# Ten multiplications of the identity by itself behind the second pair of scores in a delta-rule recurrence

## The reference

```
def step(S, inp):
    q_i, k_i, u_i, w_i = inp
    attn_i = q_i @ jnp.swapaxes(k_i, -1, -2) * mask_causal
    u_new = u_i - w_i @ S
    o_i = q_i @ S + attn_i @ u_new
    S = S + jnp.swapaxes(k_i, -1, -2) @ u_new
    return (S, o_i)
S, o = jax.lax.scan(step, S0, (to_front(q), to_front(k), to_front(u), to_front(w)))
...
o = mix * o + (1.0 - mix) * v_token
o = o * jax.lax.rsqrt(jnp.mean(o * o, axis=-1, keepdims=True) + EPS) * norm_w
```

## Time and profile before

| | us |
|---|---|
| median of 3 runs | 2300.25 |
| lowest and highest | 2298.44, 2302.13 |
| the profiled execution, its own time | 2308.04 |
| its span | 2306.2 |
| PE busy | 2047.9 |
| DVE busy | 1347.8 |
| ACT busy | 1047.4 |
| POOL busy | 631.9 |

### The profile page before, as it was taken

The page is one execution under the profiler, slowest core; times in us unless marked ns, Lnnn a source line. Parts: engine busy times, 40 slices in busy tenths (PEclk is TensorE's granted clock), DMA queues, the critical chain, the costliest instruction groups (busy, mean ns, idle before and its releaser), DMA issues. The chain is left out here.

```text
span 2306.2 us, 46308 instructions
## 1 busy us (share of the span) xinstructions
PE 2047.9 (89%) x18079; PEld 1373.9 (60%) x18079; DVE 1347.8 (58%) x3476; ACT 1047.4 (45%) x2516; POOL 631.9 (27%) x720
## 2 busy tenths in 40 slices
PE   4989999987779999698857897958999999999998
PEld 2556666656666676454535555644666666666565
DVE  2017777743545555456536883135876777766677
ACT  4235655542244444312234445344666666666322
POOL 3015930002110000103762014552333333333100
PEclk9989999987869999799965558968999999999999
DMA  2036030002010000231251013430000000000000
GB/s 66 19 27 25 2 38 2 2 18 56 13 52 3 1 1 1 81 126 22 40 135 38 2 31 90 64 88 25 1 1 1 1 1 1 1 1 2 5 14 19
DMA packets 118326, 64.37 MB, mean 28 GB/s; under 512 B 65848, under 2 KB 113248, under 8 KB 116960
## 3 DMA queue, kind: packets, MB, share of 16 engines
q1 hardware_dynamic: 106128, 52.37, 10.0%
q0 software_dynamic: 11264, 8.66, 2.6%
q10 hardware_dynamic: 720, 0.40, 0.1%
HBM read 37.54 MB, written 23.86 MB: 27 GB/s over the span
## 5 line engine op out<-in xcount | busy, mean ns | idle before, releaser
L3000 ACT ACTIVATE l_prob<-l_ps,l_neg_max 128x128 f32<-128x128 f32 (+1 forms) x512 | 208.2, 419 | 49.8 <-DVE l_neg_max L3101 45.0
L1621 ACT ACTIVATE l0a_prob<-l0a_pst 128x1024 f32<-128x1024 f32 x128 | 131.0, 1024 | 119.9 <-PE l0a_pst L1539 119.9
L2885 POOL TENSOR_TENSOR l_prob<-l_prob,l_total 128x256 f32<-128x256 f32 x128 | 78.4, 612 | 372.0 <-DVE l_total L3109 372.0
L1672 DVE TENSOR_REDUCE l0a_peak<-l0a_ps 128x4 f32<-128x1024 f32 x128 | 156.2, 1221 | 16.0 <-PE l0a_ps L1534 14.0
L1534 PE MATMUL l0a_ps<-l0a_k,l0a_q 32*128 32x256 f32 x1024 | 146.6, 406 | 3.0 <-ACT l0a_prob L1621 2.5
L644 ACT ACTIVATE l0e_hidden<-l0e_ph,l0f_b 128x512 f32<-128x512 f32 x128 | 87.9, 687 | 129.2 <-PE l0e_ph L555 129.1
L3097 DVE TENSOR_TENSOR l_ps<-l_ps,future 128x512 f32<-128x512 f32 x128 | 89.4, 698 | 97.3 <-PE l_ps L2931 97.0
L1539 PE MATMUL l0a_pst<-l0a_q,l0a_k 32*128 32x256 f32 x1024 | 145.8, 400 | 0.2 <-ACT l0a_prob L1621 0.2
L565 PEld LDWEIGHTS l0e_py<-l0f_w,l0e_hidden 128*128 128x128 f32 x1024 | 119.7, 192 | 35.0 <-ACT l0e_hidden L644 32.7
L2886 POOL TENSOR_TENSOR l_prob<-l_prob,l_total 128x512 f32<-128x512 f32 x128 | 133.0, 1039 | 0.0
L565 PE MATMUL l0e_py<-l0f_w,l0e_hidden 128*128 128x128 f32 x1024 | 129.8, 280 | 0.3 <-ACT l0e_hidden L644 0.3
(11 more groups left out here) (518 smaller groups left out, 4815.2 us busy)
## 6 DMA issues: line engine op xcount, KB each, us to landing
l_band<-zero SPq DMA_DIRECT2D x16, 272.0 KB, 6.1
x_tok<-in_x_dram SPq DMA_DIRECT2D x2, 2048.0 KB, 8.1
l2f_w<-in_L_ffn_w_dram SPq DMA_DIRECT2D x2, 2048.0 KB, 10.0
l_rows<-l_band SPq DMA_DIRECT2D x16, 256.0 KB
l1f_w<-in_L_ffn_W_dram SPq DMA_DIRECT2D x3, 1024.0 KB, 12.0
l2x_rows<-l2x_sent SPq DMA_DIRECT2D x8, 288.0 KB, 5.1
gd_tri<-gp_tri SPq DMA_DIRECT2D x8, 256.0 KB, 2.0
l0f_w<-gd_tri SPq DMA_DIRECT2D x8, 256.0 KB, 13.3
```

The source lines that it names most:

```text
L1621: act.activation(prob[:, (n // 2) % 2, pair, :, :].rearrange("p g t s -> p g (t s)"), pst[:, :, :, :].rearrange("p g t s -> p g (t s)"), A ...
L1672: dve.tensor_reduce(to, ps[m % 2][:, :, :, :], AX.X, ALU.max, negate=True).then_inc(max_ready, 1)
L3000: act.activation(prob[:, m % 4, h, cols], ps[m % 2][:, h, cols], ACT.Exp, bias=neg_max[:, m % 4, h, t:t + 1], accum_out=total[:, m % 4, h, ...
```

## The change

A helper issues `count` matmuls of the identity by the identity into a bank. It is called once in each of the seven steps that have a next chunk, behind the second pair of scores and ahead of TensorE's wait for VectorE. Each call makes ten matmuls into the first quarter of the bank `pu`. Nothing reads what they write: the next matmuls into that bank are those of `values`, which start it anew.

```
+def keep_busy(pe, c, bank, count):
+    for _ in range(count):
+        pe.matmul(bank[:, :], c.ident[:, :], c.ident[:, :], start=True, stop=True)
...
                     if t + 1 < CH:
                         pe.wait_ge(attn_saved, HEADS * (t + 1) + 2)
                         scores(t + 1, 2)
+                        keep_busy(pe, c, pu[:, 0, :], 10)
                         pe.wait_ge(attn_saved, HEADS * (t + 1) + 4)
                         if t + 2 < CH:
                             to_tokens(t + 2)
```

## The result

| | before | changed |
|---|---|---|
| median of 12 runs, us | 2301.17 | 2292.54 |
| lowest and highest | 2293.84, 2305.81 | 2287.94, 2296.33 |
| profiled execution, its own time | 2308.04 | 2292.7 |

The ratio is 0.9968, with a 95% interval of 0.9956 to 0.9981: 4 to 10 us are saved, 8.6 by the medians. The forecast was 2291.6.

The account below looks back on a forecast made before the run. PE bounds the kernel, its clock falling in each recurrence step between transposes and state matmuls. Terms -12.7 + 0.8 + 3.2 = -8.7 us, from the median 2300.25 to 2291.6 us; range 2287.0 to 2297.5.

Parts of the forecast that it names:

- a clear gain: Whole program: faster by more than 4.6 us (0.2%), chance 0.76.
- The clock's ceiling: From the transposes to the state's matmuls, seven steps: at most 12.7 us saved if all 33.2 slow busy us went.
- What falls take back: In the seven steps: two to three clock falls remain, late in a gap behind dense work, 1.3 us each, 3.2 us.
- The price of the ten: Ten added matmuls in each step's gap: 2.2 us at the high clock, 4.3 us at the low one.
- The overrun: At the high clock the ten outlast the three short gaps before the transposes, some 0.8 us in sum; four gaps hold them.
- the 7 us forecast: Sign in the changed trace: PE's waits for the second mask fall from 17.1 + 3.8 to some 7 us.
- The other parts of the stage: Recurrence outside the stretch from transposes to state matmuls and the ten's overrun: given no term in the sum.
- The rival of slow multiplications: The ten run at the low clock in every step, overrun 9.4 us onto the transposes, falls continue: 2309.7 us; chance 0.08.
- The rival by the page's rule on transposes: In every step the fall is only put off, transposes not counting as work: -2.8 us, 2297.5; chance 0.14.

Follow-up runs that it names:

- e5_again: The changed kernel as it is, timed once more; ratio to the kernel before 0.9970 (0.9960 to 0.9981).
- e7_zeros: The changed kernel with its ten matmuls multiplying zeros by zeros instead of the identity by itself; one run, 2291.88 us.
- e10: The changed kernel with 11 tiny matmuls (22 rows on PE) ahead of the first scores; ratio to the kernel before 1.0021 (1.0006 to 1.0036).
- e3_turned: The changed kernel with fifteen transposes of the identity per step instead of the ten matmuls; ratio to the kernel before 1.0002 (0.9972 to 1.0031).
- the two shifted copies: The kernel before with 11 or with 32 tiny matmuls (22 or 64 rows) ahead of the first scores; ratios to the kernel before 1.0012 and 1.0007.
- e6_wider: The changed kernel with more such matmuls ahead of the loop and around the last two turned-back outputs; ratio to the kernel before 1.0003 (0.9991 to 1.0015).
- e8_corner: The changed kernel with its ten matmuls using one corner, 32 rows by 32 columns of the identity; one run, 2300.05 us.

## Why the prediction was right

By the time, it was: 2291.6 against 2292.5 us, a saving of 8.7 against 8.6 (4 to 10), with a clear gain given a chance of 0.76. Its steps, one by one:

- **The clock's ceiling, 12.7 us.** Right. A step without a fall or a long pause needs 4.10 to 4.26 us from T to F, where 4.3 was reckoned. By the shortest steps seen, six of 4.10 and a last one of 3.3, T to F would be 27.9 us instead of 41.0: 13.1 us, an estimate.
- **What falls take back, 3.2 us by two to three of them.** The sum with the ceiling, 9.5, met the 9.8 measured, but by luck: other parts make it up. There was one fall. It came behind a pause in the second scores, not late in a long gap as reckoned, and cost 1.45 us in F to T; the T to F behind it took 4.15 us, so it cost nothing to speak of there. What T to F lost, it lost to pauses at the high clock: 1.9 us to the one in the values (5.96 instead of 4.10) and 0.85 to the one between keys and `back` (4.95 instead of 4.10, and 4.94 in e5_again). A pause had been named only as a cause of falls, not as a price of its own.
- **The price of the ten, 2.2 us at the high clock.** Right: 20 rows, the first and last start 2.22 us apart.
- **The overrun, 0.8 us, in the three short gaps.** It was 1.8 us, by how much later than 0.05 us behind the end of VectorE's mask the transposes start: 1.45 in the gap that was 1.72 us before, by the ten running slow, 0.3 in the one of 1.85, under 0.1 in the one of 2.98, and none in the one of 1.71. The waits for the mask fell to 2.6 + 1.3 = 3.9 us, further than the 7 us forecast, since pauses in the scores and in the ten took up idle time too. The gaps had been taken as fixed; but the last two short ones had been short because of a pause, and the pauses moved.
- **The other parts of the stage, cost nothing.** They lost 1.5 us ahead of the first T, where the first ten overran by 0.3, the pause at row 209 was 1.80 us instead of 0.95 and the clock was low from 525.6 to 532.4, and 0.8 in the tail, which has no ten in it. How much of this is chance is not shown; e7_zeros, with the same order of work, has 25.7 and 11.3 us there against 26.7 and 11.8.
- **The rival of slow multiplications, 0.08.** Its mechanism, a fall in the 2.5 us before the ten or 0.6 us behind their start and an overrun onto the transposes, is real: once in the changed kernel, three times in e10. I had argued that the clock is still high when the scores end; that held for the pauses where they happened to lie. The 9.4 us reckoned for seven steps is of the size of the 10.8 that three cost there. What it did not do is leave the clock low, so that e10 comes out even and not at +9.
- **The rival by the page's rule on transposes** falls with e3_turned.

So the forecast had the main mechanism and its size: the clock holds, and the path from T to F shortens. That its other terms added up was luck, and that the net was 8.6 us and not nearly zero depended on where the program's instruction count put the pauses. The prediction had no term for that.

What stays open: the typical stage of before is known from one profile, 137.7 us; its runs scatter by 12 us, and the two shifted copies, at 142.8 and 140.5, may be the more usual. The profiled execution of before points the same way: without its 10.2 us of excess in layer 2 it would have taken 2297.8 us, 3.3 below the median of 2301.17 (an estimate). That would close the distance between the 6.0 us of the profiles and the 8.6 of the timing, but it is not shown.

## What to carry to other kernels

Filling TensorE's waits with full-array work that nobody reads pays where three things hold: the work behind the wait sets the end, the granted clock is seen to fall there in each step, and the filler ends before the wait would, even at the low clock and behind a pause. Here ten multiplications left no margin for the last, and a shift of 22 rows took the gain away. Before one trusts a gain of 0.3% of this kind, the instruction count ahead of the place should be shifted and the kernel timed again.

## What the runs showed of the hardware

- **PE's pauses stand at fixed counts of rows.** They are multiples of some 127.5 matmul rows apart (847, 974, 1229, 1739, 2376, 2631 from the first score, in the changed kernel; 847, 1739 and 2631 in e6_wider and e8_corner too), and up to 4.2 us from start to start. Not every such count has a pause: before has none at 847, 974 and 1739. They repeat from run to run in place, not in length. Adding rows ahead moves them to other work: 22 rows moved the one at 209 to 187.
- **The clock goes by more than the busy share of the profile.** A fill of one 32 x 32 corner, as dense in time, left the clock at 0.79 where the full array had 0.89.
- **Zeros are enough for it.** Zeros by zeros held the clock as well as the identity (0.89 from 508 to 640 us in both). Operands without zeros were not tried.
- **32-bit transposes count.** With fifteen per step beside the other work, the clock stayed at 1.00 from 571.5 to 636 us.
